# x2 sent out early and the gated FFN added by transfers, with a shorter calibration, a new start and a split last pair

## The reference

```python
mod = (silu(c) @ wmod).reshape(16, 6, 1, 256)        # sa, ca, ga, sb, cb, gb
ga = (2*(ga >= 0) - 1) * maximum(abs(ga), 0.25)      # gb alike
h = layernorm(x) * (1 + ca) + sa
x = x + ga * attention(h)        # q, k, v, out: 256 wide with biases;
                                 # causal softmax over |q.k / 16|
h = layernorm(x) * (1 + cb) + sb
x = x + gb * ffn(h)

def calibrate(scores):           # 8 knots, piecewise linear
    pos = sigmoid(scores / (temperature + 1e-6)) * 7
    low = clip(int(pos), 0, 6)
    return knots[low] + (pos - low) * (knots[low + 1] - knots[low])
def ffn(h):
    cluster = argmax(calibrate(h @ cluster_sigs.T))              # 8 clusters
    tile = cluster * 8 + argmax(calibrate(h @ sigs.T) of that cluster)
    comp = tanh(gelu(h @ w1 + b1) @ w2 + b2)                     # 2 wide
    hh = relu(comp @ spline_w1[tile] + b[tile])                  # 16 wide
    y = h + (hh @ spline_w2[tile] + b2[tile]) * directions[tile] * output_scale
    return layernorm(y) * gamma + beta
```

## Time and profile before

| | us |
|---|---|
| median of 3 executions | 472.15 (471.57 to 474.82) |
| the profiled execution | 471.67 |
| its span on the chip | 469.8 |
| mean granted clock of TensorE in it | 0.931 of full |

### The profile page before, as it was taken

One profiled execution on the slowest core, in us unless ns is written; L12 is line 12 of the kernel. 1 busy time (PEld: TensorE's weight loads), 2 busy tenths in 40 slices (PEclk: granted clock), 3 DMA queues, 4 the chain that ended last, 5 costly groups with the idle time before them and its releaser, 6 DMA issues.

```text
span 469.8 us, 7656 instructions
## 1 busy us (share of the span) xinstructions
PE 399.8 (85%) x2072; PEld 308.7 (66%) x2072; DVE 398.5 (85%) x1367; ACT 296.5 (63%) x645; POOL 67.4 (14%) x82
## 2 busy tenths in 40 slices
PE   2697899999999999899989998999899999463330
PEld 2555578777777877687768776877677778452220
DVE  4417637387859899999999999999999899999996
ACT  2230365877698769676967697769776976651400
POOL 1002310302020002400250015001400220031040
PEclk9977899999999999999999999999999999796565
DMA  8503102101200213112310231122100210040112
GB/s 292 142 30 105 74 23 79 35 1 45 69 23 1 69 45 114 45 28 86 114 45 25 91 112 47 22 91 86 50 1 1 73 64 1 4 130 0 35 57 89
DMA packets 26234, 28.72 MB, mean 61 GB/s; under 512 B 3888, under 2 KB 21552, under 8 KB 26192
## 3 DMA queue, kind: packets, MB, share of 16 engines
q1 hardware_dynamic: 24160, 26.38, 17.8%
q10 hardware_dynamic: 2032, 1.85, 1.2%
HBM read 19.77 MB, written 8.45 MB: 60 GB/s over the span
## 4 chain that ended last, share of the span: by engine, by line
DVE 45%; PE 42%; issue 8%; ACTq 2%; ACT 2%; DVEq 0%
PE bank L511 8%; PE bank L530 8%; PE bank L490 6%; PE bank L500 6%; PE bank L553 3%; DVE y L1278 3%; DVE y L1246 3%; DVE x L1091 3%; DVE res L1288 3%; DVE st L1254 2%; DVE probs L1077 2%; DVE st L1046 2%; PE bank L520 2%; ACTq L680 2%; DVE v L1070 2%
## 5 line engine op out<-in xcount | busy, mean ns | idle before, releaser
L511 PE MATMUL bank<-h,g 128*128 128x128 f32 (+3 forms) x256 | 80.2, 444 | 4.9 <-DVE v L1070 4.9
L978 POOL TENSOR_TENSOR res<-x,gb_row 128x512 f32<-128x512 f32 x32 | 44.5, 1407 | 268.3 <-DMA out<-res 268.3
L530 PE MATMUL bank<-v,probsT 128*128 128x257 f32 x320 | 79.1, 382 | 0.0
L500 PE MATMUL bank<-m_ga,h 128*128 128x258 f32 x256 | 68.8, 394 | 5.2 <-DVE rows L1360 3.2
L530 PEld LDWEIGHTS bank<-v,probsT 128*128 128x128 f32 x320 | 57.1, 190 | 6.6 <-DVE y L1246 0.3
L490 PE MATMUL bank<-h,a_sb 128*128 128x512 f32 x128 | 60.4, 595 | 0.0
L511 PEld LDWEIGHTS bank<-h,g 128*128 128x128 f32 x256 | 44.7, 195 | 22.1 <-issue 8.5
L500 PEld LDWEIGHTS bank<-m_ga,h 128*128 128x128 f32 x256 | 47.7, 197 | 15.7 <-issue 4.3
L736 ACT ACTIVATE bank<-bank,v 128x128 f32<-128x128 f32 (+1 forms) x64 | 31.7, 495 | 41.4 <-PE bank L511 29.1
L1077 DVE CUSTOM_DVE_ANT_0 probs<-bank,cmask 128x128 f32<-128x128 f32 (+1 forms) x64 | 31.1, 485 | 23.3 <-ACT bank L736 23.3
L742 ACT ACTIVATE probs<-probs,negmax 128x128 f32<-128x128 f32 (+1 forms) x64 | 35.5, 557 | 5.9 <-DVE negmax L1077 5.9
(11 more groups left out here) (167 smaller groups left out, 770.1 us busy)
## 6 DMA issues: line engine op xcount, KB each, us to landing
x<-in_L_attn_x SPq DMA_DIRECT2D x16, 512.0 KB, 3.5
out<-res SPq DMA_DIRECT2D x16, 512.0 KB, 3.0
a_row<-gate_rows SPq DMA_DIRECT2D x16, 256.0 KB, 3.2
gb_row<-gate_rows SPq DMA_DIRECT2D x16, 256.0 KB, 3.2
wide<-in_L_wmod ACTq DMA_DIRECT2D x2, 768.0 KB, 7.6
res<-in_L_attn_Wq SPq DMA_DIRECT2D x1, 256.0 KB, 5.0
res<-in_L_attn_Wk SPq DMA_DIRECT2D x1, 256.0 KB, 7.3
res<-in_L_attn_Wo SPq DMA_DIRECT2D x1, 256.0 KB, 10.1
```

The source lines that it names most:

```text
L500: last = mm(ps[:, 0:VW], h[s][:, c, t * P:(t + 1) * P], m_ga[p % 2][s][:, c, :], start=(c == 0), stop=(c == KC - 1))
L511: last = mm(ps[:, 0:w], g[s][:, c, t * P:(t + 1) * P], h[s][:, c, 0:w], start=(c == 0), stop=(c == KC - 1))
L530: last = mm(ps[:, 0:D + 1], probsT[s][t][:, j * P:(j + 1) * P], v_sb[s][:, j, 0:D + 1], start=(j == 0), stop=(j == t))
L978: gp.tensor_tensor(res[:, 2 * u:2 * u + 2, :], x2[p % 2][s][:, t, :], gb_row[p % 2][s][:, 1:2, :].broadcast_to([P, 2, D]), ALU.add).then_i ...
```

## The change

1. **x2 and the last sum.** When x2 of a sequence is complete, SP sends it to `out` (`xo`). `ob` now adds row 1 of `gb_row` to y times rstd, so `res` holds the gated FFN alone, and GpSimd issues a transfer that adds `res` to what lies in `out` (`ay`, after `xo` has landed). So it is for groups 0 to 6 (`BY_SUM` = 7); the last two groups keep `base` and a plain `send`. New waits: `b_x2` for `xo` of p-2, `ob` for `ay` of the group before, and `ldgb` for `ob` of two groups before.
2. **Calibration.** 10 steps in place of 12. `low` is rounded once with the constant in it, and `steps` hold that constant plus j; the line's two values are not taken out by a 2x448-wide product and sum but the line is evaluated for all 7 segments and the right one is kept: three 448-wide steps and one reduce over 448.
3. **Groups.** The FFN runs over groups: pairs 0 to 6, and then the two sequences of pair 7 apart, with four tiles each. All FFN steps take a group g.
4. **Setup.** SiLU is done on the turned c. The ga rows of sequences 0 and 1 are computed on all partitions (`su_gax` on PE, `sd_gax`, `sd_gab` on DVE), without `gate_rows`; the other sequences keep the way over DRAM. Biases are loaded by GpSimd's queue, other loads go from ACT's to SP's, `wmod` comes in three parts with the first two rows ahead. The constants of the signatures (`sp_sig`) and the expert table (`sp_rest`) are made on GpSimd, some copies out of PSUM on ACT; the modulation columns of the FFN and the gb rows are made in the middle of pair 0. The steps `sd_...` and `su_...` stand between those of pair 0.
5. **Order.** The bank table and all order lists are new; they are written out in full for the first and the last pairs, with a loop for k = 5 to 7 between.

```diff
+        GROUPS = [(2 * p, 2 * p + 1) for p in range(PAIRS - 1)] + [(B - 2,), (B - 1,)]
+        BY_SUM = PAIRS - 1
...
-                need(spq, oa_rdy, PT * (p - 2) + NT * (s + 1))
-                need(spq, base_rdy, NT * (p - 2) + 2 * (s + 1))
+                    spq.wait_ge(alone_rdy, NT * (before(g - 2) + i + 1))       # ldgb
...
+            def xo(g, i):                                                      # SP
+                p, s = of_group(g, i)
+                spq.wait_ge(x2_rdy, NT * (before(g) + i + 1))
+                spq.dma_start(out_v[GROUPS[g][i]], x2[p % 2][s][:, :, :]).then_inc(x2_sent[p % 2][s], 16)
...
+            def ay(g, i):                                                      # GpSimd
+                pool.wait_ge(alone_rdy, NT * (before(g) + i + 1))
+                pool.wait_ge(x2_sent[g % 2][i], 16 * (g // 2 + 1))
+                gp.dma_start(out_v[GROUPS[g][i]], res[:, NT * i:NT * (i + 1), :], accum_op=ALU.add).then_inc(summed[i], 16)
...
             def b_x2(p, s, t):
-                need(dve, base_rdy, NT * (p - 2) + 2 * s + t // 2 + 1)
+                need(dve, x2_sent[p % 2][s], 16 * (p // 2))
...
             def ob(g, t):
+                if g < BY_SUM:
+                    if t % NT == 0:
+                        need(dve, summed[t // NT], 16 * g)
+                    rest = gb_row[g % 2][t // NT][:, 1, :]
+                else:
+                    dve.wait_ge(base_rdy, 2 * (before(g) - before(BY_SUM)) + t // 2 + 1)
+                    rest = res[:, t, :]
```

The calibration (the steps that differ; `e` becomes 1 + e^-z, `pos` is 7 / that):

```diff
-                    m(ts(low, ix, K1 - 0.6, ROUND, ALU.min, ALU.add))
-                    m(stt(out=tmp, in0=low, scalar=-ROUND, in1=ix, op0=ALU.add, op1=ALU.is_gt))
-                    m(stt(out=fl, in0=low, scalar=-ROUND, in1=tmp, op0=ALU.add, op1=ALU.subtract))
-                    m(tt(seg[:, :, :], fl.unsqueeze(2)..., steps..., ALU.is_equal))
-                    m(tt(ix, ix, fl, ALU.subtract))
-                    m(tt(seg_val[:, :, :, :], seg..., knot_lin..., ALU.mult))          # 128x896
-                    m(red(val[:, :, :], seg_val[:, :, :, :], X, ALU.add))              # over 896
-                    m(tt(ix, ix, vd, ALU.mult))
-                    m(tt(vl, vl, ix, ALU.add))
+                    m(ts(low, pos, 0.5, ROUND - 0.5, ALU.max, ALU.add))
+                    m(stt(out=back, in0=low, scalar=-ROUND, in1=pos, op0=ALU.add, op1=ALU.subtract))
+                    m(tt(own, by_segment(low), by_score(steps[:, 0:K1]), ALU.is_equal))        # 128x448
+                    m(tt(line, by_segment(back), by_score(knot_lin[:, 1, :]), ALU.mult))       # 128x448
+                    m(tt(line, line, by_score(knot_lin[:, 0, :]), ALU.add))                    # 128x448
+                    m(tt(line, line, own, ALU.mult))                                           # 128x448
+                    m(red(val[:, 0:n_], line, X, ALU.add))                                     # over 448
```

The order on GpSimd and the start of that on DVE:

```diff
-                ms(k - 1, 1)
-                base(k - 4, 2)
-                ms(k, 0)
-                base(k - 4, 3)
-                for i in range(0, 2):
-                    base(k - 3, i)
+            for i in range(0, 2):
+                ms(0, i)
+            ms(1, 0)
+            sp_sig()
+            ms(1, 1)
...
+            sp_rest()
...
+            ms(5, 0)
+            for i in range(0, 2):
+                ay(0, i)
+            ms(5, 1)
+            ms(6, 0)
+            for i in range(0, 2):
+                ay(1, i)
+            ms(6, 1)
+            ms(7, 0)
...
+            ay(6, 0)
+            for i in range(0, 2):
+                base(7, i)
+            ay(6, 1)
+            for i in range(0, 2):
+                base(8, i)
...
-            ffn_constants()
+            sd_silu()
+            sd_st(0)
+            sd_nw(0)
+            sd_col()
+            a_xh(0, 0, 2)
+            sd_st(1)
+            sd_gax(0)
+            a_xh(0, 0, 3)
+            sd_nw(1)
+            sd_vb()
+            a_h(0, 0, 1)
+            sd_bias()
+            sd_m()
...
+            sd_gab(0)
...
+            sd_gax(1)
+            sd_ga()
+            b_v(0, 0, 0)
+            sd_gab(1)
```

More of the change, by code:

```diff
@@ L675, in _ @@
+            for i in range(0, 2):
+                FS(8, i)
+            BT(7, 0)
+            HD(8)
+            OHT(7, 0)
+            CM(8)
+            for i in range(0, 4):
+                GA(7, i)
+            BT(7, 1)
+            OHT(8, 0)
+            BT(8, 0)
+            for i in range(0, 3):
+                GA(8, i)
+            BT(8, 1)
+            GA(8, 3)
         @block.scalar
@@ L1114, in _ @@
[L1114 to L1124 removed]
+                    dve.wait_ge(st2_rdy, NT * before(g + 1))
@@ new lines, in _ @@
+            oa(3, 6)
+            a_nw(7, 0)
+            clc(5, 0)
+            a_nw(7, 1)
+            clc(5, 1)
+            b_ttr(6, 1, 0)
+            b_ri(6, 0, 0)
+            clc(5, 2)
+            a_nw(7, 2)
+            b_x2(6, 0, 0)
+            b_v(6, 1, 1)
+            clc(5, 3)
+            ob(3, 4)
+            for i in range(4, 6):
+                clc(5, i)
+            b_st(6, 0, 0)
+            a_nw(7, 3)
+            b_v(6, 1, 2)
+            for i in range(6, 8):
+                clc(5, i)
@@ new lines, in _ @@
+            b_ri(6, 0, 1)
+            clc(5, 8)
+            spl(4, 0)
+            clc(5, 9)
+            for i in range(0, 2):
+                clb(5, i)
+            spl(4, 1)
+            b_ttr(6, 1, 1)
+            b_v(6, 1, 3)
+            spl(4, 2)
+            clb(5, 2)
+            b_x2(6, 0, 1)
+            spl(4, 3)
+            b_ri(6, 0, 2)
+            spl(4, 4)
+            clb(5, 3)
+            spl(4, 5)
+            b_ttr(6, 1, 2)
+            b_st(6, 0, 1)
+            y_(4, 0)
@@ new lines, in _ @@
+            clb(5, 4)
+            b_x2(6, 0, 2)
+            ob(3, 5)
+            y_(4, 1)
+            y_st(4, 0)
+            b_st(6, 0, 2)
+            b_ri(6, 0, 3)
+            pick(5, 0)
+            y_(4, 2)
+            b_x2(6, 0, 3)
+            b_ri(6, 1, 0)
+            y_st(4, 1)
+            b_st(6, 0, 3)
+            b_x2(6, 1, 0)
+            b_v(7, 0, 0)
+            b_ttr(6, 1, 3)
+            y_(4, 3)
+            pick(5, 1)
+            ob(3, 6)
+            for i in range(0, 2):
+                loc(5, i)
@@ new lines, in _ @@
+            b_ri(6, 1, 1)
+            y_(4, 4)
+            loc(5, 2)
+            b_x2(6, 1, 1)
+            oa(3, 7)
+            b_st(6, 1, 0)
+            loc(5, 3)
+            b_ri(6, 1, 2)
+            b_x2(6, 1, 2)
+            for i in range(1, 3):
+                b_st(6, 1, i)
+            ob(3, 7)
+            b_ri(6, 1, 3)
+            b_v(7, 0, 1)
+            y_st(4, 2)
+            loc(5, 4)
+            b_x2(6, 1, 3)
+            b_st(6, 1, 3)
+            for i in range(0, 3):
+                c_var(6, i)
@@ new lines, in _ @@
+            b_v(7, 0, 3)
+            lob(5, 2)
+            y_(4, 7)
+            y_st(4, 6)
+            lob(5, 3)
+            y_st(4, 7)
+            lob(5, 4)
+            for i in range(0, 3):
+                y_var(4, i)
+            oh(5, 0)
+            y_var(4, 3)
+            oa(4, 0)
+            oh(5, 1)
+            b_ri(7, 0, 0)
+            b_ttr(7, 0, 2)
+            y_nw(4, 0)
+            b_x2(7, 0, 0)
+            for i in range(1, 3):
+                y_nw(4, i)
+            for i in range(1, 3):
+                oa(4, i)
@@ new lines, in _ @@
+            clc(6, 7)
+            ob(4, 7)
+            b_ri(7, 0, 1)
+            clc(6, 8)
+            b_v(7, 1, 1)
+            clc(6, 9)
+            b_x2(7, 0, 1)
+            for i in range(0, 5):
+                clb(6, i)
+            pick(6, 0)
+            spl(5, 0)
+            b_ttr(7, 1, 0)
+            pick(6, 1)
+            spl(5, 1)
+            b_ttr(7, 1, 1)
+            spl(5, 2)
+            b_ri(7, 0, 2)
+            for i in range(3, 5):
+                spl(5, i)
+            b_x2(7, 0, 2)
@@ new lines, in _ @@
+            for i in range(1, 3):
+                b_st(7, 0, i)
+            spl(5, 5)
+            b_ri(7, 0, 3)
+            loc(6, 0)
+            y_(5, 0)
+            loc(6, 1)
+            y_st(5, 0)
+            y_(5, 1)
+            b_v(7, 1, 2)
+            b_x2(7, 0, 3)
+            y_(5, 2)
+            loc(6, 2)
+            b_st(7, 0, 3)
+            y_(5, 3)
+            y_st(5, 1)
+            y_(5, 4)
+            c_var(7, 0)
+            y_(5, 5)
+            loc(6, 3)
+            for i in range(1, 4):
+                c_var(7, i)
```

2757 lines of the change are left out of this document (1985 added, 772 removed), and 16 rows, old and new, of the table BANK.

## The result

| | before | changed |
|---|---|---|
| median, us | 471.86 | 516.56 (515.32 to 518.6) |
| ratio | | 1.094 (95% interval 1.088 to 1.101) |
| span of the profiled execution, us | 469.8 | 514.2 |

A forecast was written before the change was run, and what follows sets the result against it. PE was taken to bound the middle and DVE the tail: 333.5 to V_(7,0,0), 60.6 to the last x2, 51.6 behind it and 3.4 to the end give 449.1; 1.9 added makes 451 us, range 439 to 464.

The forecast's parts named there:

- PE takes over as the bound: Steady pairs: DVE falls from 47.5 to 44.1 us, under PE's 45.2 to 45.7; 1.8 us per pair come out.
- DVE pays for GpSimd: Steady pairs: GpSimd's `base` and `ms` hold DVE instructions, 4.6 us in one pair, 2.6 of it beside `base`.
- PE-bound middle: Main case, with a DVE-bound tail: 451 us (444 to 458), chance 0.53; V_(7,0,0) at 333.5.
- The price of an accumulating issue: GpSimd's 14 adding sends: no held DVE time taken; upper bound 1.3 us each, one DVE instruction held by 1.1.
- Rival 2: Descriptor writing holds DVE like `base`, or the start runs at low clock: 460 us (457 to 467), chance 0.20.
- Rival 5: GpSimd's queue held beyond 40 us of slack makes `ms` and V late: slower, above 477 us, chance 0.05.
- The start: Setup and pair 0: first V at 31.5, first `b_v` at 34.5 instead of 47.39, V_(1,0,0) at 69.2 instead of 78.8.
- rival 3: The start comes out whole: V at 27, 1 us lost instead of 4, no needed DVE held; 440 us, chance 0.17.
- Calibration: Twice per pair on DVE: 2.57 us occupied becomes 2.15, saving 0.42 each, 0.85 us per pair.
- The tail: After V_(7,0,0), DVE-bound: 60.6 us to the last x2, PE's 53.5 hidden, then 51.6 behind it.
- The chance of 0.04 for slower: Forecast's odds for the whole kernel: faster 0.91, same 0.05, slower 0.04.

The follow-up runs named there:

- e2: Kernel before with two table loads added to each of its 25 guesses of 1/sqrt, 67 loads against 17; 520.31 us, 1.098 of before.
- e1: Changed kernel with only ACT's table loads re-placed around gelu and tanh, 21 loads in place of 63, order kept; 469.43 us, 0.990 of before.
- e6: Kernel of e1 with Identity in place of gelu and tanh and all table loads but the first gone; 461.24 us, 0.975 of before.
- e4: Kernel before with x2 sent at once and accumulating transfers for pairs 0 to 6, old order otherwise; 461.89 us, 0.975 of before.
- e7: Kernel before with both the accumulating transfers (pairs 0 to 6) and the 10-step calibration, old order and start; 461.87 us, 0.975 of before.
- e8: Changed kernel's start, transfers and calibration, then the order and banks of the kernel before, whole pairs, 17 loads; 450.82 us, 0.956 of before.
- e3: Kernel before with the 10-step calibration alone, GpSimd sums kept; 468.7 us, 0.989 of before.
- e5: Kernel of e1 with the split of the last pair undone: eight whole pairs, steady loop run on to the end; 462.98 us, 0.979 of before.

## Why the prediction was wrong

**The step that failed is one that isn't there.** The prediction costed PE, DVE, GpSimd and SP and wrote "PE takes over as the bound" without a look at ACT's list. ACT had 36.5 of 47.5 us, its ACTIVATEs stayed nearly the same (628, then 637), and so it was taken as hidden. But the cost of an ACT list lies in its order as well as in its instructions: the diff put the next gelu between the load by hand and the Exp and Ln that this load is for. The rows of the 17 loads, 1.283 us each, were in the trace of before, and the changed order could have been held against them. That shows at least three loads a pair instead of two: the one by hand, gelu's, and that of the next Exp. The other six a pair, two for each guess, no row of before shows; they depend on the sets that the build chooses, and only the changed kernel's trace or e2 gives their number and price. Even then, ACT's 11 us of idle time would have seemed to hide them. e2 shows that it doesn't: loads inside the guess lengthen a chain that the other engines wait for. At PE's full clock 1 us of load cost 0.73 us of time, and 0.99 in the stretches where the clock fell too.

From the forecast 451 to the measured 516.6 there are 65.6 us. 47.1 went with 42 loads (e1), 8.2 more with the other 20 (e6). The 10 us that are left are the forecast's other misses. In the profiled execution of e6 they are 5.8 us less than forecast up to V1, then 0.9 more up to V3, 2.9 from V3 to V7 and 12.6 from V7 to the last `ob`. So the loads alone don't make the forecast good: with them mended the kernel takes 469.4, still above the range.

**A rule of the Trainium skill** bears on this: ScalarE: Activation LUTs, Table sets: the hidden batching unit, says to group calls by set, and that the set with exp and ln serves both with one load. The first half is what the runs show. The second holds in the kernel before, where that set was loaded by hand; in the changed kernel each of 18 pairs of Ln and Exp cost two loads. Since the Exp needed a load right behind that for its Ln, what the build loaded for the Ln can't have been used as the set with both.

**What was right, by part:**

- *Held time.* "DVE pays for GpSimd" and the sums' 2.6 us a pair: right, and a little more. In e4 the held time of a steady pair falls by 3.1 to 3.6 us, over the whole kernel from 29.6 to 6.1.
- *PE-bound middle at 45.7 to 46.* Right in mechanism and size (e4, e7, e8: 45.8), in the old order. In the new order it is 47.8 with the two loads that remain, 46.5 without. 181.2 us from V3 to V7 were forecast; e8 has 183.1, e6 184.1, e1 188.2. That e8's time is the forecast's, 451, is luck: its V1 is 1.3 us early, V1 to V7 takes 8.1 us more, and the end behind V7 7.8 less.
- *The price of an accumulating issue.* The value taken was no held time, the bound 1.3 us of GpSimd with one DVE instruction held by 1.1. Measured for the 14 in the changed kernel (ns min/median/max), and the landing of plain and adding sends (KB, us):

```profile
L1724 POOL DMA_DIRECT2D out<-res x14: 1277/1284/1388, 180.5 to 496.2; - x14
```

```profile
out<-x SPq DMA_DIRECT2D x14, 512.0 KB, 4.8
out<-res POOLq DMA_DIRECT2D x14, 512.0 KB, 6.3
```

  GpSimd is busy for the upper bound's time, but of 53 DVE instructions beside the issues one is longer than usual, by 0.22 us. Rival 2 falls. (Its price was summed wrong: 15 us less the 6 hidden, and 4 for the start, give 464 and not 460.) DMA is busy 0.33 to 0.41 of the steady stretches shown, under half as forecast. Rival 5 falls too: GpSimd's queue stood for up to 33.5 us behind an add that waited for `ob`, within the 40 us of slack, and no V waited for `m_ga`.
- *The start.* Forecast first `b_v` 34.5 and V1 69.2; measured 30.1 and 62.1. Two terms were too large. A, M and the rest were put at the low clock for 6 to 7 us more. Only A ran so (eight 256-column instructions in 3.76 us from 10.25); M's eight took 1.97 from 16.67, 0.25 each instead of 0.47, the clock's upper level. And the 4 us lost between `b_v` and V1 were none: PE is busy 35.34 of 35.40 us there. The start of rival 3 is what came.
- *Calibration.* Its 0.42 us each of DVE work has no worth in the steady part in either regime: with sums on GpSimd the held time takes most of it (e3), without them PE is the bound (e7). Behind the last x2 it gives 2.9 us in the one and 0.8 in the other.
- *The tail.* 60.6 + 51.6 = 112.2 us after V7 were forecast, as the larger of two engines' sums plus old waits. Free of switches it is 68.4 + 56.4 = 124.8 (e6), with them 131.6 (e1). The first term failed most. From V7 to the last x2 in e1 PE is busy for 64 us and DVE for 63 of 73.7: each waits for the other by turns, and the larger sum is only a lower bound. The count of the DVE list pointed the right way, 13.5 us more to do behind V7 than before, but was then set off against holds and hidden waits to 2.9 us more; e1 takes 22.3 us more than the kernel before, 27.0 more than e4.

The chance of 0.04 for slower stood on GpSimd's queue alone. It was no rival that came but a cause that none named.

**What stays open:** how much of the 10.7 us between e5 and e1 behind V7 is the split itself (twice the fixed steps on four tiles), and how much the order written for it. Which sets the build loads for Ln and Exp, and why, is open too, and so are the 5.3 us that e8 loses up to V1 against e5.

## What to carry to other kernels

When a diff changes the order on ACT, write down the sequence of function sets, not just of instructions: each change of set is a load of 1.28 us that no line of the program shows, and a load by hand is worth nothing if another set's function comes before it is used. Read the number of loads from a trace of the new order as well, since the build's choice of sets can't be read off the old one. An engine with 11 us of slack per pair is no cover for a delay inside a chain that the bound engine waits for; the slack must lie between the late result and its user. And a large change is best taken apart before it is believed: here one part (12 us) and the new start (another 11) were sound, and the order around them, with the loads that came of it, gave back nearly three times as much (516.6 against 450.8 in e8).

## What the runs showed of the hardware

- A table load on ACT is 1.283 us every time, and the next ACTIVATE starts within 0.02 us of its end where it waits for nothing else. Inside a guess most of its length came out as time (e2, V3 to V7: 30.8 us of loads, 26.5 us of time; 11.2 for 15.4 in the two stretches at full clock).
- A set that is at hand is loaded again when it is asked for by hand: e2 has 50 loads of the set that was already there, each 1.283 us.
- An accumulating transfer of 512 KB takes GpSimd 1.28 us to issue, where SP takes 0.38 for a plain one, and lands 6.3 us after it instead of 3 to 5. Beside its issue DVE is hardly held: 0.22 us in one of 53 instructions in the changed kernel; in e4 1.15 us in six of 81, which are three tensor_scalars (0.23 to 0.24 us each) and the instruction right behind each. Beside GpSimd's tensor operations, which are about as long, it was 29.6 us in 33 instructions in the kernel before.
- What GpSimd holds is decided by which DVE step lies beside it; if DVE's list gets shorter, the hold moves to another step and can grow (e3: 4.57 to 5.35 us in one stretch).
